# Third norm and gate logits moved into the self attention's end, a new routing chain, the first expert's weights fetched early, and expert rows turned by DMA

## The chip, the cores and the metric

The kernel runs on one core of one Trainium2 chip. The metric is the device time in microseconds (us) of one execution, as the median of several runs. Engines: PE (TensorE matmul), PEld (its weight loads), DVE (VectorE), ACT (ScalarE), POOL (GpSimd) and SP (SyncE, which here only issues DMA).

## What is computed

A decoder layer over 2 sequences of 512 tokens, width 512, in post-norm form. The part that the change touches is the third sub-layer, attention followed by a mixture of experts:

```python
attn_out = attention(rmsnorm(hidden_states, norm1_w), wq, wk, wv, wo)   # 16 heads of 128, 4 kv heads, causal, rope
h = hidden_states + attn_out
out = h + moe(rmsnorm(h, norm2_w), gate_w, w1, w3, w2)

def moe(x, gate_w, w1, w3, w2):            # E, F, TOPK = 8, 1024, 2
    xt = x.reshape(b * s, d)
    logits = xt @ gate_w
    topv, topi = jax.lax.top_k(logits, TOPK)
    probs = jax.nn.softmax(topv, axis=-1)
    ...                                    # w: one-hot of the two choices times probs
    for e in range(E):
        h = jax.nn.silu(xt @ w1[e]) * (xt @ w3[e])
        out = out + w[:, e:e + 1] * (h @ w2[e])
```

Before it stand a state-space layer with a layer norm and a cross attention over 1024 context tokens with a layer norm; a last layer norm stands behind it.

## The kernel before

The 1024 tokens are 8 row tiles of 128 (NT = 8; tiles 0 to 3 are sequence 0, tiles 4 to 7 are sequence 1). Every matrix product is made of three products of float16 parts, a high part (a cast, on ACT) and a low part (the value less its cast, on DVE or POOL); so "high" and "low" in the code are always ACT and then DVE or POOL. The phases run one behind the other, each in a block that ends with a barrier over all engines: the state-space layer, the cross attention ("xa"), the self attention ("sa"), `phase_norm` for the third norm, `phase_route`, a branch on whether an expert is over its capacity of 352 rows, and `phase_moe_routed`. Within a block each engine works through its own instructions in written order, and semaphores set what waits for what.

- The self attention runs over 8 halves (4 kv heads times 2 sequences) of 16 steps. A step is one query tile of one head: scores (PE, L1083), mask and minimum (DVE, L1379), exponent (ACT, L1220), a scale (POOL, L963), the high and low part of the probabilities (`sa_PN`, ACT L1198 and DVE L1347), and a DMA transpose into `sa_PT` (SP, L900). The product with the values (PE, L1095) follows six steps later, once per four steps; its result is `sa_OT` (ACT L1235, DVE L1396). The output projection is added to `X` by DVE (L1329); the last four additions are those of tiles 4 to 7.
- `phase_norm` "n3" squares each tile on ACT with a sum (L641), makes the scale on POOL (L624, L626), multiplies on DVE into `XW` (L674), transposes each tile on PE (L80) and splits it into `XT` (L86, L91). SP waits there for the norm's weights and then fetches the gate's and the first expert's weights (L597).
- `phase_route` makes the logits (PE, L1509), the two best (DVE, L1543, L1546), one-hot masks, ranks within an expert by a running sum of eight additions (L1559) and three small matmuls, and from them the rows' places: `slots`, `last_slots`, `first_at`. POOL adds `X2` (the unnormalised input) to `X` at the same time (L1501).
- `phase_moe_routed` scatters the rows to DRAM with 16 indirect DMAs of POOL (L1704). Expert 0 does not wait for them: DVE makes a 0/1 matrix `rmoe_picked` per tile (L1885) and PE multiplies the split rows with it (L1781), which gives that expert's rows already transposed. For experts 1 to 7 SP loads rows from DRAM (L1668), PE transposes them (L1740), and ACT and DVE split them into `rmoe_XGT` (L1795, L1836). An expert's up part is 8 blocks of 24 matmuls (L1753, `psG` and `psU`), its down part 3 row groups of 24 (L1768). SP's order per expert: rows of the next one, its w1 and w3 (`W13raw`, after the splits of this one), its w2 (`W2raw`, after this one's w2 splits), then the stores of the results (L1688).

## Time and profile before

| | |
|---|---|
| Time, median of 3 runs | 1512.79 us (1512.14 to 1518.51) |
| The profiled execution, time and span | 1514.51 us, span 1512.9 us |
| PE, DVE, ACT, POOL busy | 91%, 69%, 54%, 25% of the span |
| From the last addition to X to expert 0's first up matmul | 1066.2 to 1117.6 us |
| From one expert to the next | 45.40 us |

The span is what the trace covers, from the first instruction to the last. Times below are us from the span's start.

### The profile page before, as it was taken

The page shows a single profiled execution, that of the slowest core. Times are in us where ns is not written, and L with a number is a line of the kernel's source. Part 1 is how long each engine was busy: PE and PEld are TensorE (multiplying, and loading weights), DVE is VectorE, ACT ScalarE, POOL GpSimd, SP SyncE. Part 2 cuts the span into 40 slices and gives each one's busy share as a digit, 9 for nine tenths or more (in the row PEclk, how much of TensorE's full clock was granted, in tenths as well). Part 3 has the DMA queues.
Part 4 walks back from the last instruction along what each step waited for, and adds up shares of the span by engine and source line. Part 5 has one row for each costly group of instructions (what it writes and reads, how often), then busy time and mean ns, then how long its engine had stood idle before and what let it go on. Part 6 is the DMA issues. An engine that isn't in the chain of part 4 may idle for free. (4 is left out here: it accounts for less than half of the span.)

```text
span 1512.9 us, 25191 instructions
## 1 busy us (share of the span) xinstructions
PE 1372.2 (91%) x8067; PEld 734.0 (49%) x8067; DVE 1045.6 (69%) x1970; ACT 818.5 (54%) x1462; POOL 379.2 (25%) x581
## 2 busy tenths in 40 slices
PE   7988999999999999985879999998479999999991
PEld 4444444444444444432435555554246666666650
DVE  5847777777777777785678878786675554555564
ACT  4447665666666666674365656656254453444430
POOL 5402020202020101032564646542550000000044
PEclk9999999999999999996989999999689999999996
DMA  8227767575757575882634435344436354553343
GB/s 239 56 63 126 146 112 147 111 154 111 150 111 148 111 153 111 178 144 93 230 66 90 112 69 137 60 95 86 174 150 224 144 197 145 202 204 128 146 123 125
DMA packets 422079, 203.16 MB, mean 134 GB/s; under 512 B 369361, under 2 KB 383697, under 8 KB 422001
## 3 DMA queue, kind: packets, MB, share of 16 engines
q1 hardware_dynamic: 418224, 191.75, 52.2%
q0 software_dynamic: 3200, 10.49, 2.2%
q8 instruction: 34, 0.56, 0.2%
q14 instruction: 45, 0.36, 0.1%
q10 hardware_dynamic: 576, 0.00, 0.0%
HBM read 90.33 MB, written 18.55 MB: 72 GB/s over the span
## 5 line engine op out<-in xcount | busy, mean ns | idle before, releaser
L1347 DVE SCALAR_TENSOR_TENSOR X<-xa_SC,xa_rs,X 128x1024 f16<-128x1024 f32 x128 | 164.3, 1284 | 98.4 <-issue 97.7
L1198 ACT ACTIVATE X<-xa_SC,xa_rs 128x1024 f16<-128x1024 f32 x128 | 147.1, 1149 | 110.6 <-POOL xa_rs L963 110.6
L1083 PE MATMUL xa_psS<-xa_KT,xa_QT 128*128 128x512 f16 x768 | 186.4, 379 | 6.3 <-DVE xa_mn L1379 4.9
L1095 PE MATMUL xa_psO<-xa_PT,xa_V 128*128 128x512 f16 x768 | 173.7, 383 | 6.9 <-DMA xa_PT<-X 6.9
L963 POOL TENSOR_SCALAR xa_rs<-xa_rc,flag 128x1 f32<-128x1 f32 x128 | 34.2, 267 | 516.7 <-DVE xa_rc L1340 516.7
L1379 DVE CUSTOM_DVE_ANT_0 xa_SC<-xa_psS,maskb 128x1024 f32<-128x1024 f32 x128 | 154.9, 1210 | 4.5 <-PE xa_psS L1083 2.4
L1220 ACT ACTIVATE xa_SC<-xa_SC,xa_mn 128x1024 f32<-128x1024 f32 x128 | 145.5, 1136 | 13.4 <-DVE xa_mn L1379 13.3
L1768 PE MATMUL rmoe_psY<-W,rmoe_HT 128*128 128x512 f16 (+1 forms) x576 | 126.9, 379 | 0.3 <-DVE rmoe_HT L1863 0.3
L1753 PE MATMUL rmoe_psG<-rmoe_XGT,W 128*128 128x352 f16 x768 | 125.0, 313 | 1.5 <-DVE rmoe_XGT L1836 1.5
L1753 PE MATMUL rmoe_psU<-rmoe_XGT,W 128*128 128x352 f16 x768 | 125.0, 313 | 0.0
L1095 PEld LDWEIGHTS xa_psO<-xa_PT,xa_V 128*128 128x128 f16 x768 | 74.6, 99 | 101.7 <-issue 16.7
L1810 ACT ACTIVATE rmoe_SG<-rmoe_psG 128x352 f32<-128x352 f32 x64 | 29.7, 464 | 170.8 <-PE rmoe_psU L1753 170.8
L1858 DVE TENSOR_TENSOR rmoe_HF<-rmoe_psU,rmoe_SG 128x352 f32<-128x352 f32 x64 | 33.5, 524 | 126.6 <-ACT rmoe_SG L1810 126.6
L1083 PEld LDWEIGHTS xa_psS<-xa_KT,xa_QT 128*128 128x128 f16 x768 | 73.4, 98 | 90.9 <-DVE xa_mn L1379 9.6
L1220 ACT ACTIVATE sa_SC<-sa_SC,sa_mn 128x128 f32<-128x128 f32 (+3 forms) x128 | 71.5, 558 | 82.8 <-DVE sa_mn L1379 82.6
L1027 PE MATMUL xa_psJ<-XT,xa_WP 128*128 128x512 f16 x384 | 89.7, 385 | 11.4 <-POOL xa_WP L937 8.8
L1027 PE MATMUL sa_psJ<-XT,sa_WP 128*128 128x512 f16 x384 | 92.9, 396 | 7.6 <-PEq L50 5.5
L1753 PEld LDWEIGHTS rmoe_psG<-rmoe_XGT,W 128*128 128x128 f16 x768 | 75.1, 98 | 41.9 <-DVE rmoe_XGT L1836 1.9
L1753 PEld LDWEIGHTS rmoe_psU<-rmoe_XGT,W 128*128 128x128 f16 x768 | 75.1, 98 | 39.4
L1347 DVE SCALAR_TENSOR_TENSOR sa_PN<-sa_SC,sa_rs,sa_PN 128x128 f16<-128x128 f32 (+3 forms) x128 | 78.3, 612 | 21.9 <-issue 10.2
L1768 PEld LDWEIGHTS rmoe_psY<-W,rmoe_HT 128*128 128x128 f16 (+1 forms) x576 | 60.9, 106 | 60.5 <-DVE W L1861 0.7
L1051 PE MATMUL xa_psJ<-xa_WO,xa_OT 128*128 128x512 f16 x360 | 87.6, 379 | 0.0
(252 smaller groups left out, 2413.7 us busy)
## 6 DMA issues: line engine op xcount, KB each, us to landing
W13raw<-in_L_ffn_w_dram SPq DMA_DIRECT2D x16, 2048.0 KB, 11.7
W2raw<-in_L_ffn_w_dram SPq DMA_DIRECT2D x8, 2048.0 KB, 8.3
expert_rows_dram<-zeros SPq DMA_DIRECT2D x11, 512.0 KB, 9.2
xa_WPraw<-in_L_xattn_Wq_dram SPq DMA_DIRECT2D x8, 512.0 KB, 4.8
xa_WOraw<-in_L_xattn_Wo_dram SPq DMA_DIRECT2D x8, 512.0 KB, 4.6
sa_WPraw<-in_L_ffn_wq_dram SPq DMA_DIRECT2D x4, 1024.0 KB, 7.4
sa_WOraw<-in_L_ffn_wo_dram SPq DMA_DIRECT2D x4, 1024.0 KB, 5.3
expert_out_dram<-X SPq DMA_DIRECT2D x16, 256.0 KB, 2.0
```

The lines of the kernel that those rows point to most:

```text
L963: nc.gpsimd.tensor_scalar(rs[:, j % 4:j % 4 + 1], rc[:, j % 4:j % 4 + 1], unit, 1.0, ALU.mult, ALU.mult).then_inc(scale_done, 1)
L1027: last = nc.tensor.matmul(bank[:, :], wq_v[:, hw, k, a, :], XT[:, hx, k, b * S:(b + 1) * S], start=(q + k == 0), stop=(q == 2 and k == DC ...
L1051: last = nc.tensor.matmul(bank[:, :], OT[b][:, ho, g, t * P:(t + 1) * P], WO[:, hw, g, :], start=(g + q == 0), stop=(g == groups - 1 and q ...
L1083: last = nc.tensor.matmul(psS[j % NSC][:, c:c + cw], QT[b][:, hq, g, t * P:(t + 1) * P], KT[b][:, hk, c:c + cw], start=(q == 0), stop=(q = ...
L1095: last = nc.tensor.matmul(psO[:, c:], V[b][:, hv, blk, :], PT[g % NPT][:, blk, hp, c:], start=(blk + q == 0), stop=(blk == NBLK - 1 and q ...
L1198: nc.scalar.activation(PN[j % NPN][:, 0:w // P, 0, :], by_block(SC[j % NSC], w), ACT.Identity, scale=rs[:, j % 4:j % 4 + 1]).then_inc(norm ...
L1220: nc.scalar.activation(SC[j % NSC][:, 0:w], SC[j % NSC][:, 0:w], ACT.Exp, bias=mn[:, j % 4:j % 4 + 1], scale=-1.0, accum_out=sm[:, j % 4:j ...
L1347: nc.vector.scalar_tensor_tensor(out=PN[j % NPN][:, 0:w // P, 1, :], in0=by_block(SC[j % NSC], w), scalar=rs[:, j % 4:j % 4 + 1], in1=PN[j ...
L1379: nc.vector.tensor_tensor_reduce(out=SC[j % NSC][:, 0:w], in0=psS[j % NSC][:, 0:w], in1=mask_of(b, j % TPB), scale=-SCORE_SCALE, scalar=3e ...
L1753: last = nc.tensor.matmul(bank[f % 2][:, 0:CAP], W13[:, hw, w, k, f * P:(f + 1) * P], XGT[:, hx, k, :], start=(i + k == 0), stop=(i == 2 a ...
L1768: last = nc.tensor.matmul(psY[y][0:w, :], HT[:, hh, k, r * P:r * P + w], W2[:, hw, k, :], start=(i + k == 0), stop=(i == 2 and k == FC - 1))
L1858: nc.vector.tensor_tensor(HF[f % 2][:], psU[f % 2][:, 0:CAP], SG[f % 2][:], ALU.mult).then_inc(h_done, 1)
```

## The change

It makes eight edits.

1. The third norm's work goes into the self attention's block: that of tiles 0 to 3 behind the last scores, ahead of the last head's `sa_OT`; that of tiles 4 to 7 between and behind the last four additions to `X`. Its tiles are turned by 8 DMA transposes (L965 of the changed kernel) and not by PE. The gate's logits (PE, L1210) and the two best (DVE) stand at the end of the same block, so `phase_norm` "n3" with its barrier is gone.
2. The first expert's w1 and w3 are fetched in 8 DMAs of 512 KB, one behind each transpose of steps 5 to 12 of the last half; w2 is fetched in `phase_route`.
3. In `phase_route` the running sum is replaced by 28 matmuls of 8 columns, `first_at` comes from three operations fewer, and the chains for `slots` and `last_slots` go to the head of DVE's work in `phase_moe_routed`.
4. POOL's eight additions of `X2` go behind its scatters; the first copy of results of expert 0 waits for them, and so does (through a memset behind them) the load of expert 1's rows.
5. Expert 0's split rows are ready at its entry; the products with `picked` go from tile 7 to tile 0, 256 and 128 columns wide for tiles 1 and 0 in place of 352.
6. The rows that are scattered are the split ones (high and low part, the same 2 KB), and those of experts 1 to 7 are turned by three DMA transposes per expert, which SP issues behind the next w2 load. PE's transposes and the splits of rows are gone there; the up part waits for `turned`.
7. SP loads the next expert's rows behind its w1 and w3.
8. Buffers share memory (`wide`, `first`, tables that are no longer needed); this changes no operation.

The core of the diff (the two pieces that begin with `j == NS + 2` are ACT's and DVE's):

```diff
+                    if last and route is not None and 0 <= j - first_load < len(next_loads):
+                        if j == first_load:
+                            sp.wait_ge(wo_done, kv_heads * NWO)
+                            sp.wait_ge(job_ready, jobs_before(h))
+                        dst, src, arrived = next_loads[j - first_load]
+                        sp.dma_start(dst, src).then_inc(arrived, 16)
...
+            if route is not None:
+                for i in range(NT):
+                    sp.wait_ge(xp_lo, i + 1)
+                    stand_apart(sp, sp_passed)
+                    sp.dma_start_transpose(out=XT[:, :, :, i * P:(i + 1) * P].rearrange("p l k t -> p (l k) t"),
+                                           in_=XP[:, i].rearrange("p l d -> p (l d)")).then_inc(xt_in[i], 16)
...
+                    if last and route is not None and j == NS + 2:
+                        act.wait_ge(split_done, (last_h + 1) * NS)
+                        for i in range(TPB):
+                            row_square(i)
+                        for i in range(TPB):
+                            row_high(i)
...
+                    if last and route is not None and j == NS + 2:
+                        dve.wait_ge(wb_in, 16)
+                        for i in range(TPB):
+                            row_norm(i)
+                        for i in range(TPB):
+                            row_low(i)
...
+            def turn_rows(e):
+
+                sp.wait_ge(x_in, 32 * (e + 1))
+                sp.wait_ge(up_ready, FC * (e + 1))
+                stand_apart(sp, sp_passed)
+                for r in range(CTL):
+                    sp.dma_start_transpose(out=XGT[:, :, :, r * P:(r + 1) * P].rearrange("p l k t -> p (l k) t"),
+                                           in_=XR16[:, r, :]).then_inc(turned, 16)
 
             def step(e, first, last):
                 if not last:
-                    load_rows(e + 1)
                     sp.wait_ge(w13_done, 8 * (e + 1))
                     for i, w in enumerate((w1, w3)):
                         sp.dma_start(W13raw[:, i, :, :], w[bass.ds(e + 1, 1)].rearrange("o (k p) f -> p (o k) f", p=P)).then_inc(w13_in, 16)
+                    if first:
+                        sp.wait_ge(scattered, 16 * 2 * NT)
+                        sp.wait_ge(pad_zeroed, 1)
+                    load_rows(e + 1)
                     sp.wait_ge(w2_done, FC * (e + 1))
                     sp.dma_start(W2raw[:], w2[bass.ds(e + 1, 1)].rearrange("o (k p) d -> p (o k) d", p=P)).then_inc(w2_in, 16)
+                    turn_rows(e)
...
-                pe.wait_ge(tr_lo, DC * (e + 1))
+                if first:
+                    pe.wait_ge(tr_lo, DC)
+                else:
+                    pe.wait_ge(turned, 16 * CTL * e)
...
-                if not last_e:
-                    transposes(e + 1, (0, 1))
```

How the order changes, DVE at the end of the self attention. Before, the last two `sa_OT` parts stand together, and the four additions to `X` behind them:

```order
L1347 SCALAR_TENSOR_TENSOR sa_PN<-sa_SC,sa_rs,sa_PN 128x4x128
L1396 SCALAR_TENSOR_TENSOR sa_OT<-sa_psO,sa_OT 128x512 x2
L1329 TENSOR_TENSOR X<-sa_psS,X 128x512
L1329 TENSOR_TENSOR X<-sa_psJ,X 128x512 x3
L766 UNCONDITIONAL_BRANCH
```

Now (`wide` holds `XW` and its split parts):

```order
L1440 SCALAR_TENSOR_TENSOR sa_PN<-sa_SC,sa_rs,sa_PN 128x4x128
L1489 SCALAR_TENSOR_TENSOR sa_OT<-sa_psO,sa_OT 128x512
L1509 SCALAR_TENSOR_TENSOR wide<-X,sa_rr,sa_wb 128x512 x4
L1515 TENSOR_TENSOR wide<-wide 128x512 x4
L1489 SCALAR_TENSOR_TENSOR sa_OT<-sa_psO,sa_OT 128x512
L1422 TENSOR_TENSOR X<-sa_psS,X 128x512
L1422 TENSOR_TENSOR X<-sa_psJ,X 128x512
L1509 SCALAR_TENSOR_TENSOR wide<-X,sa_rr,sa_wb 128x512
L1422 TENSOR_TENSOR X<-sa_psJ,X 128x512
L1515 TENSOR_TENSOR wide<-wide 128x512
```

Eight operations of 512 columns now stand between the two `sa_OT` parts, and ACT has its four squares and four casts at the same place (L1334 and L1339 ahead of its last L1301).

SP's queue in an expert of the loop. Before (L1668 and L1670 rows, L1680 w1 and w3, L1682 w2, L1688 stores; this is expert 0's piece):

```order
L1668 DMA X<-expert_rows_dram 128x2x512
L1670 DMA X<-expert_rows_dram 96x512
L1680 DMA W13raw<-in_L_ffn_w_dram 128x4x1024 x2
L1682 DMA W2raw<-in_L_ffn_w_dram 128x8x512
L1688 DMA expert_out_dram<-X 128x512 x2
L1688 DMA expert_out_dram<-X 96x512
```

Now (`first` holds `W13raw`):

```order
L1796 DMA first<-in_L_ffn_w_dram 128x4x1024 x2
L1778 DMA X<-expert_rows_dram 128x2x512
L1780 DMA X<-expert_rows_dram 96x512
L1802 DMA W2raw<-in_L_ffn_w_dram 128x8x512
L1789 DMA_TRANSPOSE rmoe_XGT<-X 128x8x128 x3
L1809 DMA expert_out_dram<-X 128x512 x2
L1809 DMA expert_out_dram<-X 96x512
```

The three transposes stand directly behind the 2 MB of w2 in the queue, ahead of the stores.

## Rows read from the trace of the kernel before

**Rows 1.** The page: chain that ended last, share of the span by engine.
```profile
PE 24%; DVE 2%; DMA 1%; issue 0%; POOL 0%; POOLq 0%; ACT 0%
```
**Rows 2.** Windows: stretch, its length, busy us by engine, granted clock, DMA share, GB/s.
```profile
1193.50:1201.80 8.30, 8.30 (x43) 4.18 (x42) 8.07 (x12) 7.28 (x11) 0.00 (x0) 1.00 0.82 282
1056.00:1057.00 1.00, 1.00 (x6) 0.39 (x4) 0.00 (x0) 0.00 (x0) 0.00 (x0) 1.00 0.96 185
1036.00:1050.00 14.00, 14.00 (x81) 7.35 (x79) 9.52 (x30) 8.46 (x23) 1.83 (x6) 1.00 0.57 95
```
**Rows 3.** Timeline, end of the self attention: start, us, engine, line, operation.
```profile
1053.81 0.75 DVE L1347 SCALAR_TENSOR_TENSOR sa_PN<-sa_SC,sa_rs,sa_PN 128x512 f16<-128x512 f32 x1 [0.32 <-ACT sa_PN L1198]
1058.23 1.79 PE L1095 MATMUL sa_psO<-sa_PT,sa_V 128*128 128x512 f16 x12 [0.96 <-DMA sa_PT<-sa_PN]
1060.68 0.69 DVE L1396 SCALAR_TENSOR_TENSOR sa_OT<-sa_psO,sa_OT 128x512 f16<-128x512 f32 x1 [5.52 <-ACT sa_OT L1235]
1064.88 1.34 DVE L1329 TENSOR_TENSOR X<-sa_psJ,X 128x512 f32<-128x512 f32 x2 [0.60 <-PE sa_psJ L1059]
```
**Rows 4.** Timeline, third norm and two best.
```profile
1067.75 0.61 ACT L641 ACTIVATE n_sq<-X 128x512 f32<-128x512 f32 x1
1070.15 2.08 DVE L674 SCALAR_TENSOR_TENSOR XW<-X,n_rr,n_wb 128x512 f32<-128x512 f32 x3 [3.94 <-DMA n_wb<-in_L_ffn_norm_w_dram]
1076.32 0.75 POOL L624 TENSOR_SCALAR n_me<-n_ms 128x1 f32<-128x1 f32 x1
1077.15 0.55 POOL L626 TENSOR_TENSOR n_rr<-n_me,n_half 128x1 f32<-128x1 f32 x1
1083.77 2.72 PE L1509 MATMUL route_psL<-route_GWP,XT 128*128 128x8 f16 x96 [2.63 <-DVE route_GWP L1538]
```
**Rows 5.** Timeline, routing chain from the two best on.
```profile
1084.44 9.81 POOL L1501 TENSOR_TENSOR X<-X 128x512 f32<-128x512 f32 x8
1088.68 0.71 DVE L1548 TENSOR_TENSOR route_dlt<-route_top 128x8 f32<-128x8 f32 x1
1090.67 2.44 DVE L1553 TENSOR_TENSOR route_onehot<-route_expert,route_idf 128x64 f32<-128x64 f32 x2
1097.62 0.36 DVE L1575 TENSOR_TENSOR route_part<-route_onehot,route_rank 128x64 f32<-128x64 f32 x2
1100.44 0.17 DVE L1590 CAST last_slots<-route_lastf 128x8 uint32<-128x8 f32 x1
```
**Rows 6.** Timeline, entry of the routed experts.
```profile
1102.85 0.40 DVE L1885 TENSOR_SCALAR rmoe_picked<-rmoe_row,first_at 128x352 f16<-128x352 f32 x1 [2.25 <-POOL rmoe_row L1700]
1103.23 1.75 POOL L1704 DMA_INDIRECT expert_rows_dram<-XW,slots  x1 [0.41 <-issue]
1104.00 1.33 PE L1781 MATMUL rmoe_psT<-rmoe_picked,XT 128*128 128x352 f16 x4 [7.50 <-DVE XT L1887]
1126.13 1.33 POOL L1704 DMA_INDIRECT expert_rows_dram<-XW,slots  x1 [0.30 <-issue]
1117.56 1.96 PE L1753 MATMUL rmoe_psG<-rmoe_XGT,W 128*128 128x352 f16 x12 [1.50 <-DVE rmoe_XGT L1836]
```
**Rows 7.** Timeline, expert 0's down part and SP's w2 loads.
```profile
1146.21 0.77 PE L1740 MATMUL rmoe_psT<-identF,X 128*128 128x128 f32 x6
1146.82 5.34 PE L1768 MATMUL rmoe_psY<-W,rmoe_HT 128*128 128x512 f16 x24
1162.97 1.95 PE L1753 MATMUL rmoe_psG<-rmoe_XGT,W 128*128 128x352 f16 x12
1148.13 0.37 SPq L1682 DMA_DIRECT2D W2raw<-in_L_ffn_w_dram  x1
1193.53 0.37 SPq L1682 DMA_DIRECT2D W2raw<-in_L_ffn_w_dram  x1
```
**Rows 8.** DMA issues: KB each, median us from issue to landing.
```profile
W2raw<-in_L_ffn_w_dram SPq DMA_DIRECT2D x8, 2048.0 KB, 8.3
sa_PT<-sa_PN SPq DMA_TRANSPOSE x128, 2.7
```

More of the change, by code:

```diff
@@ L1148, in _ @@
                     last_output(t, [groups - 1])
+                pe.wait_ge(gw_done, 1)
+                for i in range(NT):
+                    pe.wait_ge(xt_in[i], 16)
+                    for q, (hx, hw) in enumerate(PAIRS):
+                        for k in range(DC):
+                            logits = nc.tensor.matmul(psL[i // TPB][:, i % TPB * E:(i % TPB + 1) * E], XT[:, hx, k, i * P:(i + 1) * P],
+                                                      GWP[:, hw, k, :], start=(q + k == 0),
+                                                      stop=(q == 2 and k == DC - 1))
+                    if i % TPB == TPB - 1:
+                        logits.then_inc(logits_ready, 1)
             else:
@@ L1625, in phase_moe_routed @@
         first_bank = psT + psY
-        picked = sb("picked", [P, NT, CAP], F16)
-        row = sb("row", [P, CAP], F32)
-        XP = XT[:].rearrange("p l k t -> p (l k t)").rearrange("p (l t d) -> p l t d", l=2, d=D)
+        slots = sb("slots", [P, 2, NT], U32)
+        slotf = sb("slotf", [P, 2, NT], F32)
+        part = sb("part", [P, 2, NT, E], F32)
+        lastf = sb("lastf", [P, 2, NT], F32)
+        last_slots = sb("last_slots", [P, NT], U32)
         Y1, Y2 = XW, XT[:].rearrange("p l k t -> p (l k t)").bitcast(F32).rearrange("p (t d) -> p t d", d=D)
@@ L1770, in step @@
                     last.then_inc(down_ready, 1)
-                    if r == 0 and not last_e:
-                        transposes(e + 1, (2, 3))
-            for t in range(NT):
-                pe.wait_ge(picked_done, t + 1)
-                pe.wait_ge(xp_lo, t + 1)
+            for n, t in enumerate(reversed(range(NT))):
+                w = min(CAP, (t + 1) * P)
+                pe.wait_ge(picked_done, n + 1)
                 for k in range(DC):
                     for hx in range(2):
-                        last = nc.tensor.matmul(first_bank[k][:, 0:CAP], XP[:, hx, t, k * P:(k + 1) * P], picked[:, t, :],
-                                                start=(t + hx == 0), stop=(t == NT - 1 and hx == 1))
-                    if t == NT - 1:
+                        last = nc.tensor.matmul(first_bank[k][:, 0:w], XP[:, t, hx, k * P:(k + 1) * P], picked[:, t, 0:w],
+                                                start=(n + hx == 0), stop=(t == 0 and hx == 1))
+                    if t == 0:
                         last.then_inc(tr_ready, 1)
@@ new lines, in decoder_layer @@
+        with ExitStack() as cross:
+            CT = cross.enter_context(nc.sbuf_tensor("CT", [P, 2, DCTX // P, B * S2], F16))
+            maskb = cross.enter_context(nc.sbuf_tensor("maskb", [P, B, S2], F32))
+            weights, loads = attention_weights(nc, cross, "xa", 2, DCTX // P, xWq, xWk, xWv)
+            phase_ssm(nc, X, XT, CT, x, ctxt, mask, W_in, W_out, log_A, W_dt, b_dt,
+                      (identF, causal, maskb, flag, ropeC, ropeS, zeros), rope_in, weights, loads, X2, wide, first)
+            attention(nc, "xa", X, XT, CT, identF, weights, xWq, xWk, xWv, xWo, 8, 2, S2,
+                      lambda b, t: maskb[:, b, :], flag, None, ready=True, turned=wide,
+                      tail=(norm1_w, X2, (own_raw, own_split, own_in), own_loads, own_wo[:, 0, :]))
```

397 lines of the change are left out of this document (231 added, 166 removed).

## The prediction

> **What bounds the kernel now.** I read the chain first: PE holds nearly all of what the page resolves of it, so time is saved where PE works less or waits less [rows 1]. Then I went through the timeline from the self attention's end. The last addition to X ends at 1066.2 (1064.88 and 1.34) [rows 3] and expert 0's first up matmul is at 1117.56 [rows 6]: 51.3 us in which DVE, ACT and POOL make a serial chain and PE does little of lasting use. Behind that, an expert is 45.40 us long (from one w2 load to the next) [rows 7] and PE is never idle in it. So the change has two places: the chain of 51.3 us, and PE's transposes in seven experts.
>
> **Self attention's end.** DVE's last low part ends at 1054.56; from there DVE waits 5.52 us for its part of the last head's sa_OT, which runs from 1060.68 to 1061.37 [rows 3]. Into this gap go the norms of tiles 0 to 3. Four squares at 0.61 end near 1057.1; the scale on POOL (0.2 to 0.75, then 0.55) near 1058.2; four multiplications at 0.69 (2.08 for three) near 1061.0 [rows 4]; four low parts, taken at 0.67 like the additions (1.34 for two), near 1063.7; only then comes sa_OT, until 1064.4. It is 3.0 us late, and the output projection and the four additions stand behind it. The work does not fit the gap.
>
> The 4 MB of w1 and w3 lie in the same stretch. A 2 MB load is 8.3 us at a DMA share of 0.82, so 6.8 us of all engines; twice that is 13.6. In 1036 to 1050 the share is 0.57, which leaves 6.0 of 14 [rows 2]. The other 7.6 push the probabilities' transposes back. With 3.2 us for the last three transposes (590 KB at 185 GB/s [rows 2]) the last one lands near 1060.5, where the value product now starts at 1058.23, behind a wait of 0.96 for just that landing [rows 3]. This runs beside the norm work, and mostly hides under it: I take 4.1 us for both; the bounds are 3.0 (loads hidden) and 6.5 (both in full).
>
> Then tiles 4 to 7. The last addition would end at 1070.3. Three operations of tiles 4 and 5 stand ahead of it on DVE (2.1, and 0.2 of waits): 1072.6. Behind it five operations of 0.68 alternate with ACT's squares and casts, 4.9 with the waits: 1077.5. A DMA transpose alone lands in 2.7 at the median [rows 8]; this one is larger than their mean (256 KB, against 160), 3.0: 1080.5. Twelve matmuls are 0.34 (2.72 for 96) [rows 4]. The copy, four maxima and four indices are 1.4 (eight took the time up to 1088.68 [rows 5]). The barrier between two blocks is 0.9 (the norm's first square, 0.6 ahead of the second at 1067.75 [rows 4], against 1066.2). So route_dlt stands at 1083.5, where it is now at 1088.68: **gain 5.2**, between 2.8 and 6.5. Nothing is gained from fetching the weights early: they now come behind the norm and arrive unnoticed.
>
> **Routing.** From route_dlt to last_slots there are 11.9 us, up to 1100.61. Until 1094.25 POOL adds X2 (9.81 for eight), and DVE's operations of 64 columns take 1.22 each (2.44 for two), where the same size takes 0.18 once POOL is silent (0.36 for two) [rows 5]. The first five are 5.7 us and become 1.1. The running sum and its clearings, 1.7, give way to 29 matmuls at 0.028, 0.85, and the wait for them; the slots and last_slots chains, 2.5, leave. What stays is about 4.0: **gain 7.9**, between 6.5 and 8.5. The two taken-out chains come back in front of the expert 0 splits of DVE: 2.9 for the picked rows, 1.9 for the chains, 4.6 for four w13 splits, 9.4 in all, ahead of PE's 11.2; without that cover they would cost 1.9. The barrier and branch, 1.8 up to the picked rows' block, stay.
>
> The slow operations are a rule of the Trainium skill too (SBUF — State Buffer, "Who interferes with whom"): a DVE instruction with two SBUF inputs is locked out while a GpSimd one reads SBUF. The trace agrees, 1.22 against 0.18. The rule speaks against where the additions go, beside expert 0's up part, and that gives a rival below.
>
> **Entry.** picked starts at 1102.85 behind POOL's iota, PE at 1104.00, and the up part at 1117.56 [rows 6]. PE's 64 products end 1.5 ahead of the up part, so they hold 12.06 us. The first four take 1.33, where the up part's twelve of the same width take 1.96, so 0.65 for four: PE is at half its rate behind an idle stretch, and stays so about as long as now. The iota wait goes (0.5), the split ahead of PE's first product goes (0.6), and 19,968 columns replace 22,528, which is 0.9 to 1.2 less at the fast rate: **gain 2.0**, between 0.5 and 3.
>
> **Experts 1 to 7.** PE's twelve transposes per expert hold it 0.61 twice (1146.21 to 1146.82, and the second group alike) [rows 7]: 1.22, and seven times that is **8.5**. That is had only if the turned rows are there in time. The w2 load is issued at 1148.13 and the next up part starts at 1162.97, so 14.84 later; without the transposes 13.6 later [rows 7]. The load lands after 8.3 [rows 8]; three transposes of 256 KB behind it are 786 KB, at 185 GB/s [rows 2] 4.25 us. Together 12.55, and some tenths for the landing: 0.7 to 1.0 us to spare. I take them as hidden; the bounds are 8.5 and, if each trio is 1 us slower than that margin, 1.5. The row loads wait behind 4 MB of weights, but the up part is 28.6 long, so they are early. ACT and DVE lose 3 us of work per expert, which PE did not wait for. SP's stores of results wait behind three more issues; the next who needs their buffers is an expert later.
>
> **POOL.** The scatters run from 1103.23 to 1127.4, 24.2 [rows 6]. They start at about 1093.5 now, end at 1117.7, and the additions end at 1127.5. Expert 0's first copy of results is due near 1136, and the rows of expert 1 are wanted by 1133. Nothing in the sum.
>
> **Sum.** 5.2 + 7.9 + 2.0 + 8.5 = 23.6. The profiled execution took 1514.5, so 1490.9; it stood 1.7 over the median, so 1489 as a median.
>
> **Rivals.**
> *Rows turned late by a little.* The margin is under 1 us in 13.6 and rests on a rate from transposes that came alone. If a trio takes 1 us more than the margin allows, 7 us of the 8.5 are gone: 1496. With the upper bound of the attention's end as well, 1499. For it: everything in the queue stands behind 2 MB. Against: the gap between the load's end and the due time is 5.3 us for 4.25 of transfers.
> *Transposes one by one.* If each begins only when the one before has landed, three cost 3.2 each (2.7 scaled to 256 KB) behind the 8.3, 17.9 in all, 4.3 late, seven times: 30 us, more than the sum: 1519. This is slower by over 0.5% from 3.25 us each on. For it: nothing in the kernel turns three tiles at once behind a large load. Against: a landing is 2.7 while 256 KB hold the DMA engines for 1.4, so they overlap.
> *The additions' lock.* POOL's adds beside expert 0 can hold DVE's two operations with two SBUF inputs per block for up to 1.2 each, so 1.7 becomes 4.2 per block, over PE's 3.58, in four blocks: 2.5 late, less two blocks of lead, and rows of expert 1 some 5 us later. Once, 0 to 3: 1491. This is what the rule of the SBUF page, named above, would make of it.
> *The attention's end is not paid for.* If ACT's four squares and DVE's eight operations take the last gap at less than counted (the squares fit into earlier waits) the gain there is up to 3 more: 1485.
>
> **How the numbers follow.** Forecast with its hidden transposes, the lock's once-only cost with it: 0.63, own range 1484 to 1494. Rows a little late: 0.22, 1494 to 1501. Better at the attention's end or the entry: 0.08, 1479 to 1484. One by one: 0.04, 1513 to 1530. Something in the attention's end that costs over 8 us: 0.03, about 1503 to 1508. Leaving out the last two and part of the third gives 1482 to 1500. A measurement tells about 0.5%, 7.6 us, from no change; so faster holds the first three cases and a little more, 0.93, same 0.04, slower 0.03.
>
> **What the profile of after would show.** Right: sa_OT of the last head at 1063 to 1066 with ACT's squares ahead of it; no DVE operation over 0.3 in the routing; the first up matmul 13 to 17 us earlier, near 1102; from one w2 load to the next 44.2; no wait of PE for `turned`. Wrong: PE idle before the first up matmul of each expert, with a DMA as releaser (then the rate or the queue order is wrong); an entry that is short but an attention that ends over 6 us later; granted clock under 1.0 in the experts, which no term here allows for.

## The result

The changed kernel takes 1501.42 us (median of 5, 1497.71 to 1503.51), the kernel before 1515.78 beside it: ratio 0.9905, 95% interval 0.9881 to 0.9929. Timed again, beside other kernels, it was 1501.06 against 1513.87 (0.9914, 0.9899 to 0.9928). The forecast was 1489. So the change is a gain of 13 to 14 us where 23.6 were worked out.

The profiled execution of the changed kernel (1497.71 us, span 1496.0) was the fastest of its five. Its span is 16.9 us under that of before. Where they come from, from one landmark to the next, each read in the timelines of both:

| from | to | before | after | gained | forecast |
|---|---|---|---|---|---|
| start | mask of the last scores (DVE) | 1050.69 | 1049.14 | 1.55 | 0 |
| there | route_dlt | 37.99 | 33.45 | 4.54 | 5.2 |
| there | PE's first product with picked | 15.32 | 6.14 | 9.18 | 9.0 |
| there | first up matmul | 13.56 | 12.11 | 1.45 | 0.9 |
| there | first w2 load of the experts | 30.57 | 39.23 | **-8.66** | 0 |
| there | seventh w2 load | 272.41 | 265.08 | 7.33 | 7.3 |
| there | end | 92.36 | 90.85 | 1.51 | 1.2 |

(The 9.0 and 0.9 are the routing's 7.9 and the entry's 2.0, of which 1.1 lie ahead of the first product.) All rows but two are within 0.7 us of their term. The first row has no term in the sum; in the executions of the runs below that mask stands anywhere between 1048.3 and 1051.4, so its 1.55 tells nothing of the change. The other is expert 0's up part, which the sum gave nothing.

Timeline of the changed kernel, end of the self attention and routing: the rows that answer to [rows 3 to 6].
```profile
1052.59 1.79 PE L1151 MATMUL sa_psO<-wide,sa_V 128*128 128x512 f16 x12 [3.67 <-DMA wide<-sa_PN]
1059.40 1.79 PE L1151 MATMUL sa_psO<-wide,sa_V 128*128 128x512 f16 x12
1059.03 2.74 DVE L1509 SCALAR_TENSOR_TENSOR wide<-X,sa_rr,sa_wb 128x512 f32<-128x512 f32 x4 [3.29 <-POOL sa_rr L1068]
1061.69 2.49 DVE L1515 TENSOR_TENSOR wide<-wide 128x512 f16<-128x512 f32 x4
1064.09 0.68 DVE L1489 SCALAR_TENSOR_TENSOR sa_OT<-sa_psO,sa_OT 128x512 f16<-128x512 f32 x1
1082.59 0.17 DVE L1667 TENSOR_TENSOR route_dlt<-top 128x8 f32<-128x8 f32 x1 [1.28 <-PEq L50]
1083.17 0.45 DVE L1671 TENSOR_TENSOR onehot<-route_expert,route_idf 128x64 f32<-128x64 f32 x2
1088.73 1.36 PE L1895 MATMUL rmoe_psT<-rmoe_HT,wide 128*128 128x352 f16 x4 [3.52 <-DVE rmoe_HT L1999]
```
The eight operations of 512 columns stand where the order put them, and the last sa_OT is 4.96 us later behind the last mask than before (14.95 against 9.99; forecast 4.1). PE's wait of 3.67 for a transpose of probabilities is new, and beside it lie the 512 KB loads. In the routing, two one-hot operations take 0.45 in place of 2.44 [rows 5].

The same kernel in expert 0: POOL's additions, DVE's low part of w2 beside them, and PE's up part; then windows of PE (columns as in [rows 2]).
```profile
1113.45 0.96 POOL L1824 DMA_INDIRECT expert_rows_dram<-wide,rmoe_slots  x1 [0.30 <-issue]
1114.43 9.83 POOL L1827 TENSOR_TENSOR X<-X 128x512 f32<-128x512 f32 x8
1110.89 0.75 DVE L1967 TENSOR_TENSOR W<-W2raw,W 128x512 f16<-128x512 f32 x1
1114.47 10.34 DVE L1967 TENSOR_TENSOR W<-W2raw,W 128x512 f16<-128x512 f32 x1
1100.84 2.77 PE L1871 MATMUL rmoe_psG<-rmoe_XGT,W 128*128 128x352 f16 x12 [2.06 <-DVE rmoe_XGT L1941]
1106.11 1.95 PE L1871 MATMUL rmoe_psG<-rmoe_XGT,W 128*128 128x352 f16 x12
1125.74 3.62 PE L1871 MATMUL rmoe_psG<-rmoe_XGT,W 128*128 128x352 f16 x12 [5.15 <-DVE zeros L1964]
```
```profile
1100.80:1106.00 5.20, 5.16 (x24) 2.94 (x25) 4.63 (x4) 2.97 (x4) 4.29 (x4) 0.67 0.42 162
1125.70:1129.20 3.50, 3.46 (x13) 1.79 (x14) 2.57 (x5) 1.84 (x4) 0.00 (x0) 0.51 0.58 206
1129.20:1133.00 3.80, 3.80 (x27) 2.52 (x26) 1.32 (x3) 1.45 (x3) 0.00 (x0) 1.00 0.00 0
```
One DVE instruction, 0.7 us long in the other blocks, takes 10.34: it begins with the eight additions and ends with them. PE runs out of work, is idle for 5.15, and then runs one group of 12 at half its rate (3.62 for 1.95; granted clock 0.51, so the 1.2 GHz level). That is 6.8 of the 8.66. The other 1.7 are the first two groups, 2.77 and 2.87 for 1.95 each, at half the clock for part of the way behind 2.06 us of idleness.

In `again`, a second timing of the same kernel with a trace of its own, the first group takes 1.96, but two groups behind the hold are slow:
```profile
1126.27 3.70 PE L1871 MATMUL rmoe_psG<-rmoe_XGT,W 128*128 128x352 f16 x12 [5.66 <-DVE zeros L1964]
1129.76 3.05 PE L1871 MATMUL rmoe_psU<-rmoe_XGT,W 128*128 128x352 f16 x12
```
So its up part is 39.20 too. And its entry, from the first product with picked to the first up matmul, takes 13.20 and not 12.11, since more of those products run at half the clock. Over all executions the two go together: an entry of 12.0 to 12.3 is followed by slow first groups, one of 12.5 to 13.5 by a first group of 1.96 or 1.97. So 1.1 of the 1.7 stands on the other side in the entry, whose gain is 1.45 in this trace and 0.4 in `again`.

Back in the first trace of the changed kernel, SP between two experts and the next up part: the rows that answer to [rows 7].
```profile
1140.07 0.37 SPq L1802 DMA_DIRECT2D W2raw<-in_L_ffn_w_dram  x1
1184.25 0.37 SPq L1802 DMA_DIRECT2D W2raw<-in_L_ffn_w_dram  x1
1184.82 9.52 SPq L1789 DMA_TRANSPOSE rmoe_XGT<-X  x3
1197.87 1.95 PE L1871 MATMUL rmoe_psG<-rmoe_XGT,W 128*128 128x352 f16 x12
```
From load to load there are 44.18 us, 1.22 less than before, and PE does not wait for `turned`.

### The profile page after: what moved, and what is told of

Read it like the earlier page. It is cut to its first block and busy times, and to the rows that moved or that the text cites. A ratio compares the mean times of both kernels' runs of the same rounds, so it can differ in the third digit from the quotient of the medians.

```text
span 1496.0 us, 24896 instructions
## 1 busy us (share of the span) xinstructions
PE 1357.0 (91%) x7985; PEld 720.3 (48%) x7985; DVE 1031.8 (69%) x1920; ACT 804.4 (54%) x1426; POOL 375.2 (25%) x578
## 5 line engine op out<-in xcount | busy, mean ns | idle before, releaser
L1151 PE MATMUL xa_psO<-wide,xa_V 128*128 128x512 f16 x768 | 173.3, 383 | 8.6 <-DMA wide<-X 8.6
L1286 ACT ACTIVATE xa_SC<-xa_SC,xa_mn 128x1024 f32<-128x1024 f32 x128 | 145.4, 1136 | 14.8 <-DVE xa_mn L1472 14.7
L1151 PEld LDWEIGHTS xa_psO<-wide,xa_V 128*128 128x128 f16 x768 | 74.5, 98 | 103.8 <-issue 18.4
L1083 PE MATMUL sa_psJ<-XT,first 128*128 128x512 f16 x384 | 92.0, 393 | 7.9 <-PEq L50 5.5
L1264 ACT ACTIVATE sa_PN<-sa_SC,sa_rs 128x128 f16<-128x128 f32 (+3 forms) x128 | 71.0, 555 | 29.4 <-POOL sa_rs L1001 24.6
L1107 PE MATMUL sa_psJ<-sa_WO,sa_OT 128*128 128x512 f16 x336 | 77.1, 379 | 9.0 <-DVE sa_OT L1489 5.9
```

What stands on the lines that cost most here:

```text
L1083: last = nc.tensor.matmul(bank[:, :], wq_v[:, hw, k, a, :], XT[:, hx, k, b * S:(b + 1) * S], start=(q + k == 0), stop=(q == 2 and k == DC ...
L1107: last = nc.tensor.matmul(bank[:, :], OT[b][:, ho, g, t * P:(t + 1) * P], WO[:, hw, g, :], start=(g + q == 0), stop=(g == groups - 1 and q ...
L1151: last = nc.tensor.matmul(psO[:, c:], V[b][:, hv, blk, :], PT[g % NPT][:, blk, hp, c:], start=(blk + q == 0), stop=(blk == NBLK - 1 and q ...
L1264: nc.scalar.activation(PN[j % NPN][:, 0:w // P, 0, :], by_block(SC[j % NSC], w), ACT.Identity, scale=rs[:, j % 4:j % 4 + 1]).then_inc(norm ...
L1286: nc.scalar.activation(SC[j % NSC][:, 0:w], SC[j % NSC][:, 0:w], ACT.Exp, bias=mn[:, j % 4:j % 4 + 1], scale=-1.0, accum_out=sm[:, j % 4:j ...
```

## The experiments

All were timed in five rounds beside the kernel before. "Hold" is the longest DVE low part of w2 in expert 0, "up" the time from the first up matmul to the first w2 load (30.57 before).

| run | median, range | ratio, interval | hold | up |
|---|---|---|---|---|
| again | 1501.06 (1500.58 to 1502.68) | 0.9914 (0.9899 to 0.9928) | 10.86 | 39.20 |
| no_adds | 1492.87 (1488.92 to 1493.43) | 0.9851 (0.9833 to 0.9869) | 0.69 | 30.57 |
| spaced | 1494.78 (1494.04 to 1496.23) | 0.9870 (0.9855 to 0.9886) | 2.33 | 30.57 |
| between | 1493.30 (1492.72 to 1496.17) | 0.9868 (0.9852 to 0.9885) | 0.88 | 32.25 |
| in_route | 1497.20 (1495.92 to 1503.12) | 0.9893 (0.9875 to 0.9910) | 0.69 | 30.57 |
| groups4 | 1495.58 (1494.84 to 1496.92) | 0.9884 (0.9869 to 0.9900) | 5.99 | 32.62 |
| four_parts | 1501.13 (1495.88 to 1504.32) | 0.9915 (0.9895 to 0.9934) | 9.83 | 39.47 |
| start_free | 1496.68 (1496.07 to 1502.95) | 0.9897 (0.9880 to 0.9915) | 1.53 | 35.24 |
| start_caught | 1496.81 (1493.75 to 1500.94) | 0.9887 (0.9870 to 0.9904) | 1.53 | 33.77 |
| gap | 1506.83 (1504.96 to 1509.50) | 0.9874 (0.9854 to 0.9893) | 1.33 | 31.11 |
| caught_scatter | 1510.36 (1508.41 to 1512.06) | 0.9896 (0.9880 to 0.9912) | 10.46 | 36.21 |
| late_fetch | 1491.91 (1490.88 to 1492.81) | 0.9850 (0.9834 to 0.9866) | 2.35 | 30.58 |
| low_behind | 1491.33 (1485.02 to 1491.89) | 0.9837 (0.9816 to 0.9858) | 1.59 | 30.58 |
| all_three | 1490.55 (1490.14 to 1492.66) | 0.9853 (0.9837 to 0.9868) | 1.80 | 32.25 |
| all_between | 1490.99 (1489.09 to 1492.61) | 0.9851 (0.9835 to 0.9867) | 0.89 | 32.25 |
| turns4 | 1495.14 (1492.43 to 1496.19) | 0.9865 (0.9845 to 0.9885) | 2.34 | 30.58 |

gap and caught_scatter ran where the kernel before took 1526.84, so they are compared by their ratio. In start_free, start_caught and caught_scatter the additions also end some 9 to 14 us later. SP's w2 load stands behind the rows of expert 1, which wait for them, so "up" is longer there; in start_free and start_caught PE is not idle in it.

### Are the additions the loss?

**no_adds** leaves the eight additions out (its output lacks the unnormalised input).
```diff
-            for i in range(NT):
-                nc.gpsimd.tensor_tensor(X[:, i, :], X[:, i, :], X2[:, i, :], ALU.add).then_inc(x_added, 1)
+            pool.sem_inc(x_added, NT)
```


> The changed kernel without POOL's eight additions of X2 to X (they are left out, so the residual is missing from the output); POOL counts x_added up by 8 at once. Theory (lock): in the changed kernel one DVE split of w2 is held 10.3 us by the additions, PE idles 5.15 us and runs its next block at half rate (1.7). Without them the stretch from expert 0's first up matmul (1100.8) to its w2 load (1140.1), 39.2 us, falls to about 32.3, no DVE operation there is over 1.3, and the time falls by 6.5 to 7. Rival (data): the stall comes from transfers beside expert 0 (scatters, 4 MB of weights); then the stretch stays near 39 and the time within 1 us.

**spaced** puts a semaphore wait behind each addition.
```diff
                 nc.gpsimd.tensor_tensor(X[:, i, :], X[:, i, :], X2[:, i, :], ALU.add).then_inc(x_added, 1)
+                pool.wait_ge(x_added, i + 1)
```


> The changed kernel, where POOL waits for each of its eight additions to end before it starts the next. Theory (starving): DVE is held for as long as additions follow each other without a gap; with a gap between them DVE gets in after one, 1.2 us, as the 64-column operations did in the routing of the kernel before. The longest DVE split is 2 us or less, PE's idle time beside expert 0 under 1 us, the time 5 to 7 us less. Rival (one lock after another): the order is set by who asks first at each end, the gap of a semaphore changes nothing, the split stays near 10 us and the time the same. Rival (data): no change.

**between** makes each addition behind a pair of scatters.
```diff
                                             in_=XPF[:, t, :], in_offset=None).then_inc(scattered, 16)
+                nc.gpsimd.tensor_tensor(X[:, t, :], X[:, t, :], X2[:, t, :], ALU.add).then_inc(x_added, 1)
-            for i in range(NT):
-                nc.gpsimd.tensor_tensor(X[:, i, :], X[:, i, :], X2[:, i, :], ALU.add).then_inc(x_added, 1)
```


> The changed kernel with one addition behind each second scatter of POOL, so that single additions of 1.2 us lie between scatters from 1091 to 1125. Theory (lock): each holds DVE at most 1.2 us, DVE has 1 to 2 us to spare per block, PE idles under 0.5 us for it; the additions near 1093 to 1099 delay the splits ahead of the first up matmul by up to 2 us, and the time is 5 to 7 us less than the changed kernel's. Rival (sum of locks): eight additions cost DVE 10 us wherever they stand, and PE waits as long in total: time within 2 us of the changed kernel's.

**in_route** has the additions in the routing, as before the change.
```diff
             pool.wait_ge(row_done, 1)
+            for i in range(NT):
+                nc.gpsimd.tensor_tensor(X[:, i, :], X[:, i, :], X2[:, i, :], ALU.add)
```


> The changed kernel with the eight additions back in the routing phase, behind POOL's small operations, as the kernel before has them. Theory (lock): expert 0's stretch falls to 32.3 as without additions, and the routing's operations of 64 columns that fall under the additions take 1.2 instead of 0.2 to 0.45: idf, two onehot, picks and those behind, 8 to 9 operations, so the routing is 5 to 9 us longer. Net within 3 us of the changed kernel. Rival: if the routing stays at 4 us, the slow operations of the kernel before had another cause, and the time is 7 us less.

Without the additions the up part is 30.57 again and the time 8.2 to 8.6 us under that of the changed kernel. I had expected 32.3 and 6.5 to 7; the difference is that the first two groups ran at the full rate in this execution. Where they were slow, as in between, the same part is 32.25. So the hold and the slow groups behind it are worth 7.0 of the 8.66 (39.23 less 32.25), and all of the 8.6 in again. The same additions with a wait behind each cost little (spaced), and so do single ones between the scatters (between), against the rival of a sum of locks: their work isn't the loss, the unbroken row is. In timelines, spaced (first two rows) and in_route (the others):
```profile
1118.96 2.33 DVE L1967 TENSOR_TENSOR W<-W2raw,W 128x512 f16<-128x512 f32 x1
1119.45 12.55 POOL L1827 TENSOR_TENSOR X<-X 128x512 f32<-128x512 f32 x8
```
```profile
1085.61 9.79 POOL L1637 TENSOR_TENSOR X<-X 128x512 f32<-128x512 f32 x8
1085.83 1.07 DVE L1682 TENSOR_TENSOR p<-route_ex,p 128x8 f32<-128x8 f32 x1
1097.37 1.35 PE L1896 MATMUL rmoe_psT<-rmoe_HT,wide 128*128 128x352 f16 x4 [10.91 <-DVE rmoe_HT L2000]
```
In spaced DVE's low part is held for the first addition and gets in at the wait behind it. In in_route the row is unbroken too, yet a DVE instruction with two SBUF inputs is held for one addition only (1.07 for 0.17). There the loss is another: POOL does not reach the block's end until 1095.4, so PE starts 7.4 us later behind the rank matmuls than in no_adds (12.07 against 4.69), and most of what expert 0 saves is lost again.

### What decides whether the hold lasts for one addition or for all?

**groups4** has one wait, behind the fourth addition.
```diff
+                if i == 3:
+                    pool.wait_ge(x_added, 4)
```


> The changed kernel with one semaphore wait, between the fourth and the fifth of POOL's additions. Theory (a low part of 128 x 512 on DVE that starts beside unbroken additions is held until the last one of the unbroken row is over): the longest low part is near 5 us and not 10.3, PE, which has 5.2 us of work ready there, waits 0 to 1 us, and the time is 1494 to 1497, as with a wait behind each addition. Rival (each DVE operation is delayed by some share of all eight additions, wherever it starts): the longest is still over 8 us and the time stays at 1501.

**four_parts** makes DVE's low part of w2 in four instructions of 128 columns.
```diff
-                    nc.vector.tensor_tensor(dst[:, 1], src, dst[:, 0], ALU.subtract).then_inc(w2_done, 1)
+                    for c in range(0, D, P):
+                        part = nc.vector.tensor_tensor(dst[:, 1, c:c + P], src[:, c:c + P], dst[:, 0, c:c + P], ALU.subtract)
+                    part.then_inc(w2_done, 1)
```


> The changed kernel, its eight additions unbroken, but each low part of w2 on DVE is made as four instructions of 128 columns in place of one of 512 (twice as much per low part in all experts by the fixed cost of an instruction, about 0.3 us more for each, which PE does not wait for). Before the change, the routing's operations of 64 columns took 1.22 each beside the same additions, one addition long. Theory A (what is held until the end is an instruction as such, whatever its size): one part takes some 10 us, time 1501. Theory B (a small instruction slips in behind one addition, a large one does not): four parts of 1.2 each, no instruction over 2 us, PE waits 0 to 2 us, 1495 to 1498.

Timelines, groups4 first, then four_parts:
```profile
1116.09 5.99 DVE L1969 TENSOR_TENSOR W<-W2raw,W 128x512 f16<-128x512 f32 x1
1122.01 1.58 DVE L1971 TENSOR_TENSOR rmoe_HT<-causal,rmoe_HT 128x352 f16<-128x352 f32 x1
1124.08 1.96 PE L1873 MATMUL rmoe_psG<-rmoe_XGT,W 128*128 128x352 f16 x12 [1.87 <-DVE zeros L1966]
```
```profile
1116.42 9.81 POOL L1827 TENSOR_TENSOR X<-X 128x512 f32<-128x512 f32 x8
1116.56 9.83 DVE L1968 TENSOR_TENSOR W<-W2raw,W 128x128 f16<-128x128 f32 x1
```
The hold follows the length of the row (5.99 for four additions), and it is no matter of size: an instruction of 128 columns, 0.27 us long, was held for 9.83, against my theory B. The second row of groups4, just as unbroken, held each instruction for one addition only (1.58 for 0.52).

In all these holds the DVE instruction was in progress, or just began, when the row began. **start_free** and **start_caught** put `pool.wait_ge(h_lo, 5)` or `pool.wait_ge(h_done, 5)` ahead of the additions.

> The changed kernel, its eight additions unbroken, but POOL waits ahead of them until DVE has finished the last operation of expert 0's fifth up block (h_lo at 5), so that no DVE operation with two SBUF inputs runs when the first addition begins. Theory (only an instruction that is caught in progress, or starts within 0.2 us, by the first addition is held for the whole row; one that starts later waits for the addition in progress): the low parts beside the additions take 1.2 to 2.4 us each, PE waits 0 to 1 us, 1494 to 1497. Rival (unbroken additions hold the first such DVE instruction until their end, whenever it starts): a low part of 7 to 8 us, PE idle for some 3 us and at half rate behind it: 1499 to 1501.

> The same with the wait for DVE's first operation of that block (h_done at 5), directly behind which its low part of w2 begins. Theory: that low part is caught by the first addition and takes 9.8 to 10.6 us, PE is idle for some 5 us: 1500 to 1502. Rival (the start does not matter, and the changed kernel's hold came by chance of alternation): 1.2 to 2.4 us as in the other kernel, and 1494 to 1497.

Neither holds anything throughout, so the theory of the caught instruction fell. Their times, 1496.7 and 1496.8, lie where no hold was expected to put them, but partly by luck: both lose time elsewhere. The additions now end so late that PE waits 4.04 and 3.64 us for the first turned rows of expert 1. In start_free:
```profile
1150.06 3.70 PE L1872 MATMUL rmoe_psG<-rmoe_XGT,W 128*128 128x352 f16 x12 [4.04 <-DMA rmoe_XGT<-X]
```
**gap** and **caught_scatter** ask whether the scatters ahead of the row matter.
```diff
+            nc.gpsimd.memset(half[:], -0.5).then_inc(half_done, 1)
+            pool.wait_ge(half_done, 1)
             for i in range(NT):
                 nc.gpsimd.tensor_tensor(X[:, i, :], X[:, i, :], X2[:, i, :], ALU.add).then_inc(x_added, 1)
```
```diff
                 for k in range(2):
+                    if t == NT - 1 and k == 0:
+                        pool.wait_ge(h_lo, 5)
```
gap comes first, then caught_scatter.

> The changed kernel with one small memset and a semaphore wait between the last scatter and the first addition; the eight additions stay unbroken. Theory (what holds an instruction throughout is a row of additions that begins directly behind an indirect DMA): no low part over 2.4 us, PE not idle in expert 0, 1494 to 1497. Rival (only the moment decides: the row begins within half a microsecond of a low part's start, which 0.2 us hardly changes): a low part of about 10 us, 1500 to 1502.

> The changed kernel, but the last two scatters wait until DVE has finished expert 0's fifth up block (h_lo at 5). The low part of the next block begins 2.5 us after that and the additions, directly behind the two scatters, some 2.6 us after it, so they meet as in the changed kernel but 8 us later. Theory (as above): a low part of about 10 us. PE has two blocks ready there, so the loss is up to 5 us again: 1499 to 1502; if the additions miss the low part by more than half a microsecond it is held for one addition only and tells nothing. Rival (it was something else of the changed kernel's moment): 1.2 to 2.4 us, 1495 to 1497.

The closest pair, in timelines, start_caught first, then caught_scatter:
```profile
1121.94 0.69 DVE L1968 TENSOR_TENSOR W<-W2raw,W 128x512 f16<-128x512 f32 x1
1122.04 12.52 POOL L1828 TENSOR_TENSOR X<-X 128x512 f32<-128x512 f32 x8 [6.79 <-DVE causal L1965]
1122.55 1.59 DVE L1970 TENSOR_TENSOR rmoe_HT<-causal,rmoe_HT 128x352 f16<-128x352 f32 x1
```
```profile
1127.01 0.96 POOL L1826 DMA_INDIRECT expert_rows_dram<-wide,rmoe_slots  x1 [0.31 <-issue]
1127.99 9.84 POOL L1829 TENSOR_TENSOR X<-X 128x512 f32<-128x512 f32 x8
1127.92 10.46 DVE L1969 TENSOR_TENSOR W<-W2raw,W 128x512 f16<-128x512 f32 x1
1138.96 0.81 PE L1886 MATMUL rmoe_psY<-W,rmoe_HT 128*128 128x512 f16 x3 [1.69 <-DVE rmoe_HT L1971]
```
In both, the low part begins 0.1 us ahead of the row. Behind a semaphore wait it takes its 0.69 and the next instruction is held for one addition; directly behind an indirect DMA it is held for all eight. (The time shows little of it, 0.9896 against 0.9874 in gap, because PE had only its down part to start: it is idle for 1.69 and then twice for 0.70.) Over all traces: five rows that came directly behind a scatter and met a low part at their beginning held it to their end (changed kernel, again, four_parts, groups4's first, caught_scatter); of six unbroken rows that did not come directly behind one (before, in_route, groups4's second, start_free, start_caught, gap) none did. But only two of the six met a low part in progress: start_caught's, and groups4's second, where the held low part got in at the wait and was still running for 0.5 us when the fifth addition began. The contrast rests on these two. In in_route the first instruction with two SBUF inputs began 0.22 behind the row, in gap 2.09, in start_free 2.37 and in before 4.24.

What makes the difference is narrowed down and not shown. In start_caught too POOL's last instruction ahead of the row is an indirect DMA, but a semaphore wait stands between, 6.79 us long. So start_caught and caught_scatter differ in whether POOL goes on from the DMA to the row without a wait. Whether it matters that it is a DMA, no run shows: none has a row that comes without a wait behind another instruction and meets a low part in progress. Whether a row behind a scatter would hold an instruction that starts later in it, no run shows. A side effect: a row that takes turns with DVE is longer, 11.8 to 12.5 us for eight in place of 9.8.

### The attention's end

**late_fetch** issues the eight loads behind the last transpose of probabilities, **low_behind** moves the casts and low parts of tiles 0 to 3 behind the last sa_OT, both on top of spaced; **all_three** is both, and **all_between** is both on top of between.
In late_fetch, SP behind its loop over the steps:
```diff
+                if last and route is not None:
+                    sp.wait_ge(wo_done, kv_heads * NWO)
+                    sp.wait_ge(job_ready, jobs_before(h))
+                    for dst, src, arrived in next_loads:
+                        sp.dma_start(dst, src).then_inc(arrived, 16)
```
In low_behind, DVE (and ACT's casts likewise):
```diff
-                        for i in range(TPB):
-                            row_low(i)
...
                 output_add(h, 1, t, jobs_before(h) + JO + t, acc[t])
+                if route is not None:
+                    for i in ((0, 1), (2, 3), (4,), (5,))[t]:
+                        row_low(i)
```


> A semaphore wait stands behind each of POOL's additions of X2 (worth about 6.6 us, as measured before, 1494.8), and besides the eight loads of w1 and w3 are issued behind the self attention's last transpose of probabilities and not between its last twelve. Theory: the early loads hold these transposes up, so without them PE's wait of 3.7 us ahead of head 14's value product goes, the norms of tiles 0 to 3 start 2.3 us earlier and route_dlt comes 2 us earlier: 1492.8. Rival: the normed rows' eight transposes then stand behind 4 MB in the DMA queue (13.6 us for the weights and 11 for the rows in a stretch of 22) and the logits end 1 to 3 us later: 1496 to 1498. A third: neither, since the norm work hides it: 1494.8.

> The same waits behind the additions, and besides the casts (ACT) and low parts (DVE) of the normed tiles 0 to 3 come behind the last head's sa_OT, the low parts two at a time behind the first two output additions, and not ahead of it. Theory: they hold the last sa_OT back by 2.3 us (PE's last value product is over at 1061.2 and DVE starts its part at 1064.1), so it comes 2.3 us earlier and so does route_dlt: 1492.5. Rival: the four low parts, 2.5 us, then delay the output additions as much as they delayed sa_OT: 1494.8, with sa_OT earlier and route_dlt where it was.

> The three repairs together: a wait behind each of POOL's additions, the loads of w1 and w3 behind the last transpose of probabilities, and the casts and low parts of tiles 0 to 3 behind the last head's sa_OT. If their effects add (late fetch about 2.9, the moved low parts about 3.5 against the waits alone at 1494.8): 1488 to 1489. If both only make room for the same wait (the DMA's landing, then sa_OT): 1491. If the normed rows' transposes, issued nearer to the weights, become the bound: over 1493.

> The same, but with the additions one by one behind each pair of scatters in place of the waits. With the waits alone or the interleaving alone the medians were 1494.8 and 1493.3, so 0 to 1.5 us under the run above: 1487 to 1491. Its DVE low parts should stay under 1 us, as they did alone.

Timelines of late_fetch, then all_three:
```profile
1050.60 1.79 PE L1149 MATMUL sa_psO<-wide,sa_V 128*128 128x512 f16 x12
1064.09 0.68 DVE L1487 SCALAR_TENSOR_TENSOR sa_OT<-sa_psO,sa_OT 128x512 f16<-128x512 f32 x1
1083.66 0.17 DVE L1665 TENSOR_TENSOR route_dlt<-top 128x8 f32<-128x8 f32 x1 [1.28 <-PEq L50]
```
```profile
1060.78 0.68 DVE L1487 SCALAR_TENSOR_TENSOR sa_OT<-sa_psO,sa_OT 128x512 f16<-128x512 f32 x1
1069.49 0.44 PE L1208 MATMUL sa_psS<-sa_GWP,XT 128*128 128x8 f16 x12 [3.91 <-DMA XT<-wide]
1082.24 0.17 DVE L1664 TENSOR_TENSOR route_dlt<-top 128x8 f32<-128x8 f32 x1 [1.28 <-PEq L50]
```
PE's wait of 3.67 is gone in the three runs with the late fetch, and stands at 3.2 to 4.2 in the others, so the early loads made it. Measured from the mask of the last scores (1050.98 in late_fetch, 1050.42 in low_behind, 1050.09 in all_three), the last sa_OT begins at 13.11, 14.04 and 10.69; in the executions without either edit at 14.8 to 16.9, before the change at 9.99. Both causes are real, and only together do they give back the 4.3 us between the profiled execution of the changed kernel and all_three. Of these little reaches the end: route_dlt stands at 32.68, 33.74 and 32.15, without the edits at 33.3 to 36.0. In all_three 1.2 of the 4.3 go between sa_OT and the last low part of tile 7 (13.44 us in place of 12.23), where the moved low parts stand between the additions to X. Another 1.75 go from there to route_dlt (8.02 in place of 6.27), where the logits wait for the DMA transposes of the normed rows. Whether these are late for standing behind the weights or because all eight now follow each other closely, no run separates.

The wait that the early loads make has a second price, the clock. The product of head 14, the last but one, with the values stands behind it. Its row in groups4, and then its windows in groups4 and in the changed kernel (columns as in [rows 2]):
```profile
1053.03 3.36 PE L1151 MATMUL sa_psO<-wide,sa_V 128*128 128x512 f16 x12 [3.63 <-DMA wide<-sa_PN]
1053.00:1056.40 3.40, 3.37 (x13) 1.78 (x14) 0.75 (x1) 0.59 (x1) 0.00 (x0) 0.50 1.14 299
1052.60:1054.40 1.80, 1.80 (x13) 1.13 (x14) 0.75 (x1) 0.55 (x1) 0.00 (x0) 1.00 1.05 344
```
Only in the changed kernel's first trace and in between does it run at full rate (1.79); these two have the earliest sa_OT, 14.95 and 14.78. In the other twelve executions with early loads it takes 2.1 to 3.4, low_behind's too (3.02), and route_dlt comes up to 2.8 later. With the late fetch it takes 1.79 in all three.

The medians of all four are 1490.6 to 1491.9, the least of all kernels, about 22 us under the kernel before. They are 2.9 to 4.2 us under spaced, but the intervals of the ratios meet: a gain of either edit over spaced is likely and not settled, and that both gains add up was not seen.

### The margin of the turned rows

**turns4** adds a fourth transpose per expert into an unused buffer, on top of spaced.
```diff
+                sp.dma_start_transpose(out=XGD[:, :, :, 0:P].rearrange("p l k t -> p (l k) t"),
+                                       in_=XR16[:, 0, :]).then_inc(turned, 16)
```


> The same waits behind the additions, and besides a fourth transpose of 256 KB per expert behind the three, into a buffer that nobody reads, and PE waits for all four. Now the DMA engines fall silent 0.8 us ahead of the next up part. Theory (the transfers overlap, each costs 1.4 us at the rate of the queue): PE waits 0.6 per expert, seven times 4: 1499, between 1497 and 1501. Rival 1 (each trio is paced by SP's issue, 9.6 us for three, 3.2 each): PE waits 2.4 per expert: 1512. Rival 2 (the slack is larger than it looks): no wait, 1494.8.

PE's waits in turns4 from 1140 to 1440 (releaser: us in total, times, longest):
```profile
PE rmoe_psG L1875 <- DMA rmoe_XGD<-X: 0.4, 1, 0.4
```
A fourth transpose costs 0.4 us, once in seven experts, and the time stays at spaced's. So rival 2 was nearest: the margin was about one transfer of 256 KB and not 0.8. SP's 9.5 us for issuing three transposes is not their pace, since the fourth was issued in 1.33.

## Why the prediction was wrong

- **The step that failed** is the part "POOL": "Nothing in the sum." It looked only at when the additions end, and who waits for them. The additions' lock was named as a rival, at "up to 1.2 each" and "0 to 3" once. The price per instruction came from [rows 5], where each DVE operation is held for one addition. The row behind the scatters held one instruction for eight, 10.34 us: PE was idle for 5.15 and 1.7 more went at half the clock. In [rows 5] the additions begin at 1084.44 and the first DVE instruction with two SBUF inputs, route_dlt, at 1088.68, so those rows could not show what happens to one that is in progress when the additions begin. My "up to 1.2 each" was taken for a bound, and it was none. With the 7.0 of the hold and the slow group behind it taken off, the sum is 16.6, beside the 16.9 of the span.
- **The rivals.** The rival of rows turned late reached 1501, about the time measured, but by something that did not happen: PE never waits for `turned`. The nearness is luck.
- **The Trainium skill's rule** (SBUF — State Buffer, "Who interferes with whom"), that a DVE instruction with two SBUF inputs is shut out while a GpSimd one reads SBUF, pointed at the right place. By what it says of whole instructions the hold is one addition, which the traces show in other rows (1.59 for 0.52); for a row behind an indirect DMA the measurement, eight additions, decides.
- **The attention's end** came within 0.7 us, 4.54 for 5.2. sa_OT was 4.96 late and not 4.1. Both causes that I named, the norm's operations and the loads, were shown, and that they mostly hide under each other too (all_three); the norm's work alone made it 3.1 late (late_fetch) for the 3.0 of the sum. One reading was wrong: DVE's wait of 5.52 begins at 1055.16 and not at 1054.56, because the sa_OT of head 14, the last but one, stands behind the last low part and takes 0.68. With both edits together (all_three) route_dlt came only 1.3 us earlier, since the transposes of the normed rows are next in line. And the 4.54 are those of an execution at full clock; the same instructions in again gained 3.86, and in the executions with the half-rate product down to 2.0.
- **Routing and entry** held: 10.63 for 9.9 (9.53 in again). In the routing no operation is over 0.46, where I had said 0.3.
- **Experts 1 to 7** held to the hundredth, 44.18 per expert. "0.7 to 1.0 us to spare" was on the careful side, since turns4 has room for one transpose more.
- **The clock.** I allowed nothing for it. The first two up groups ran at half of it for a part in some executions (2.77 and 2.87), 1.7 us, and not in others of the same kernel (1.96 and 1.95 in again), whose entry was 1.1 longer. Behind the hold it cost 1.7 in one and 2.85 in the other.
- **From span to median.** The terms that were off make 6.7 us in the span. The rest of the 12.4 is that I took 1.7 off for the median, where the profiled execution of the changed kernel was 3.7 under its own. The 1.7 was itself an accident of three runs: against the median of five, 1515.78, the profiled execution of before stood 1.3 under.

Open: whether it is the indirect DMA directly ahead of the row or the missing semaphore wait that makes the hold last, and why; and how much of the 2.8 us by which the attention's end varies between executions of the same instructions (route_dlt at 33.3 to 36.0) is the clock. Head 14's product alone varies by 1.6 (1.79 to 3.36).

## What to carry to other kernels

When work of POOL is moved, ask what DVE does beside it, and take the price of a lock from a row in which POOL does the same things in the same order: here the same eight additions cost a DVE instruction one addition's time in one place and all eight in the other. A semaphore wait between POOL's instructions, which left expert 0's up part as short as without the additions (30.57), gave 6.6 us back. Look as well at what DVE has in progress when such a row begins. And a gap in which PE or DVE waits has a second user already, the DMA queue: what is put into it must be looked at in both.

## What the runs showed of the hardware

- Directly behind an indirect DMA, with no semaphore wait between, an unbroken row of POOL additions held one DVE instruction to its end: 10.34, 10.86, 9.83 and 10.46 us for eight, 5.99 for four. Six rows that did not follow one directly held none for more than one addition; two of the six met an instruction in progress, and both had a semaphore wait directly ahead.
- Behind 5.15 and 5.66 us of idleness PE ran a group of 12 in 3.62 and 3.70, at a granted clock of 0.5; behind 4.04 (start_free) in 3.70; behind 1.87 (groups4) in 1.96. Behind 2.06 us it ran at half the clock in some executions and at full in others, and behind 3.2 to 4.2 us in the self attention too (12 of 512 columns in 3.36 at a clock of 0.50, or in 1.79 at 1.00).
